# Inflows of a selective scan on GpSimd: two tiles of channels in one instruction

## The reference

```python
delta = jax.nn.softplus(jnp.einsum('blr,dr->bld', dt_r, dt_proj_w) + dt_proj_bias)
A = -jnp.exp(A_log)
def step(h, inp):
    delta_t, B_t, C_t, x_t = inp
    dA = jnp.exp(delta_t[..., None] * A)
    h = h * dA + (delta_t * x_t)[..., None] * B_t[:, None, :]
    y_t = jnp.einsum('bdn,bn->bd', h, C_t)
    return (h, y_t)
```

## Time and profile before

| | us |
|---|---|
| median of 3 runs | 2214.0 |
| lowest and highest run | 2208.6, 2216.2 |
| span of the profiled execution | 2212.1 |
| scan stage in it (`mamba`) | about 60 to 1310 |
| VectorE busy in the span | 1611.7 |
| TensorE busy in the span | 1779.5 |
| GpSimd busy in the span | 1009.2 |
| ScalarE busy in the span | 793.1 |

### The profile page before, as it was taken

How to read it: one execution, slowest core, us unless ns; L and a number is a source line. 1 busy time by engine, 2 the same in 40 slices (tenths; PEclk the granted TensorE clock), 3 DMA queues, 4 the chain that set the end, 5 groups by cost and what they waited for, 6 DMA issues and landing times. The chain is left out here.

```text
span 2212.1 us, 31372 instructions
## 1 busy us (share of the span) xinstructions
PE 1779.5 (80%) x8084; PEld 1285.4 (58%) x8084; DVE 1611.7 (73%) x2184; ACT 793.1 (36%) x1172; POOL 1009.2 (46%) x777
## 2 busy tenths in 40 slices
PE   3778767687676876768866668979997999999998
PEld 3345544454434554445543435657786999999997
DVE  0369999999989999899998834335763566655664
ACT  0444555445464553645545401211001233332332
POOL 1057547676576764767756532000001444433443
PEclk9989879798897997879978888999998999999999
DMA  5111101111101120011201042221121656666564
GB/s 135 69 29 64 53 25 35 39 58 56 29 30 40 54 64 24 30 40 49 69 25 30 24 162 85 95 106 57 58 79 44 163 124 165 162 146 164 143 161 82
DMA packets 81603, 169.61 MB, mean 77 GB/s; under 512 B 22459, under 2 KB 27467, under 8 KB 77979
## 3 DMA queue, kind: packets, MB, share of 16 engines
q1 hardware_dynamic: 57360, 116.06, 15.6%
q0 software_dynamic: 17856, 44.85, 10.4%
q10 hardware_dynamic: 6187, 6.37, 1.1%
HBM read 261.62 MB, written 39.24 MB: 136 GB/s over the span
## 5 line engine op out<-in xcount | busy, mean ns | idle before, releaser
L789 POOL TENSOR_TENSOR dbx<-u,b_all 128x512 f32<-128x512 f32 x512 | 642.2, 1278 | 350.5 <-DVE h L687 345.2
L687 DVE TENSOR_TENSOR_SCAN h<-da,dbx 128x512 f32<-128x512 f32 x512 | 596.2, 1203 | 40.2 <-ACT da L587 40.2
L587 ACT ACTIVATE da<-delta,a_neg 128x504 f32<-128x504 f32 x512 | 347.9, 684 | 474.1 <-DVE h L687 469.2
L427 PE MATMUL hT<-ident,h 128*128 128x128 f32 x2048 | 313.5, 313 | 229.6 <-DVE h L687 229.0
L427 PEld LDWEIGHTS hT<-ident,h 128*128 128x128 f32 x2048 | 274.8, 163 | 342.9 <-issue 337.6
L700 DVE SCALAR_TENSOR_TENSOR yacc<-hT,c_now,yacc 128x512 f32<-128x512 f32 x480 | 331.4, 732 | 4.3 <-PE hT L427 4.2
L334 PE MATMUL bank<-hid,w_in 128*128 128x512 f32 x608 | 291.4, 627 | 7.6 <-ACT hid L467 7.6
L1921 POOL DMA_INDIRECT out<-y,slots_kept x76 | 135.6, 1784 | 226.4 <-issue 158.1
L334 PEld LDWEIGHTS bank<-hid,w_in 128*128 128x128 f32 x608 | 120.4, 207 | 137.0 <-issue 128.1
L1554 POOL DMA_DIRECT2D slots_kept<-lists_kept x1 | 0.6, 577 | 331.2 <-DVE lists_kept L1508 331.2
L394 PE MATMUL bank<-w_out,skip 128*128 128x512 f32 x320 | 147.7, 609 | 2.5 <-DVE skip L659 2.5
(11 more groups left out here) (234 smaller groups left out, 3312.7 us busy)
## 6 DMA issues: line engine op xcount, KB each, us to landing
w_up_kept<-in_up_T SPq DMA_DIRECT2D x76, 1408.0 KB, 6.1
w_dn_kept<-in_dn_T SPq DMA_DIRECT2D x76, 768.0 KB, 7.4
b_all<-bt_scratch SPq DMA_DIRECT2D x128, 256.0 KB, 3.2
x_in<-in_x_pad ACTq DMA_DIRECT2D x21, 256.0 KB
res<-in_x_pad SPq DMA_DIRECT2D x20, 256.0 KB, 3.7
x_scratch<-res SPq DMA_DIRECT2D x20, 256.0 KB, 3.4
w_in<-in_in_T SPq DMA_DIRECT2D x8, 512.0 KB, 4.7
x_in<-x_scratch SPq DMA_DIRECT2D x4, 1024.0 KB, 5.3
```

Source lines behind the costliest of these rows:

```text
L427: mm = nc.tensor.transpose(hT[t][:, d * P:(d + 1) * P], h[:, m % RING, d, t * P:(t + 1) * P], ident[:])
L587: nc.scalar.activation(out[:, :, 1:], rows[:, :, 1:], ACT.Exp, scale=a_neg[:, d, n:n + 1]) \
L687: nc.vector.tensor_tensor_scan(h[:, n % RING, i, :], da[i % RING][:], dbx[:, i, :], 0.0, ALU.mult, ALU.add).then_inc(scan_done, 1)
L789: nc.gpsimd.tensor_tensor(dbx[:, i, :], u[:, d, :], b_all[:, m % RING, :], ALU.mult) \
```

## The change

One GpSimd instruction now makes the inflows of two neighbouring tiles of channels, 128x1024 columns: u of two tiles, times b_all repeated over both (`broadcast_to`, no copy is made). Per step two such instructions take the place of four. Each waits until the scans of the step before are done for both of its tiles, and at n = 0 until u of both is there. It adds 2 to dbx_made when it is done, so the semaphore's values mean what they meant, and no other engine's code changes.

```diff
+PAIR = 2
@@ inflow
                 if n == 0:
-                    pool.wait_ge(u_ready, j * DT + d + 1)
+                    pool.wait_ge(u_ready, j * DT + d + PAIR)
                 if i == 0:
                     pool.wait_ge(b_full[m % RING], j * (16 * STEPS // RING) + 16 * (m // RING + 1))
-                pool.wait_ge(scan_done, j * SCANS + HT * m + i + 1)
-                nc.gpsimd.tensor_tensor(dbx[:, i, :], u[:, d, :], b_all[:, m % RING, :], ALU.mult) \
-                    .then_inc(dbx_made, 1)
+                pool.wait_ge(scan_done, j * SCANS + HT * m + i + PAIR)
+                both = b_all[:, m % RING, :].unsqueeze(1).broadcast_to([P, PAIR, BLK])
+                nc.gpsimd.tensor_tensor(dbx[:, i:i + PAIR, :], u[:, d:d + PAIR, :], both, ALU.mult) \
+                    .then_inc(dbx_made, PAIR)
@@ the loop
                 for m in range(STEPS):
-                    for i in range(HT):
+                    for i in range(0, HT, PAIR):
                         inflow(j, *divmod(m, NST), i)
```

## The result

| | us |
|---|---|
| changed kernel, median of 4 runs | 2295.8 (2291.5 to 2300.3) |
| kernel before, beside it, median of 4 runs | 2214.3 (2208.6 to 2216.2) |
| ratio | 1.038 (95% interval 1.035 to 1.040) |
| spans of the profiled executions | 2298.0, before 2212.1 |

The change costs 82 us; 72 were forecast (2286 against 2296). Between the first and the last scan of the block loop the two traces differ by 83 of the 86 us of their spans, so the loss lies in the scan stage.

A forecast was written before the change was run, and what follows sets the result against it. VectorE was taken as the bound in the scan stage. Stalls of 19.4 us per block less 1.4 absorbed by waits gave 18.0, over four blocks 72 us, hence 2286 us, range 2253 to 2318.

The forecast's parts named there:

- What bounds: Scan stage: VectorE sets the pace, GpSimd's inflows lie beside its work, and VectorE never waits for dbx.
- The lock: A VectorE instruction with two SBUF inputs meeting a GpSimd TENSOR_TENSOR stands until its end, then needs 0.55 us.
- three-operand instructions: Rival: L625 and L633 share with GpSimd and don't stand; 5.4 us per block, 2236 us; chance 8%.
- a lock that falls between the tiles: Rival: GpSimd gives way in the middle of the pair, so stalls shrink; 2198 us; chance 6%.
- The price of the pair: One 128x1024 inflow on GpSimd takes 2.37 us, where two of today's take 2.51 us.
- the first three lines of the table: Stalls behind the last additions: 0.99 us in each of 11 steps, 0.63 in four, 0.52 in two.
- m = 31: Last step of a block: GpSimd itself waits for the next block's u, so nothing changes; 0 us.
- m = 0: Block's first scans, with L659 meeting the pairs and c_now's copy ending 0.1 us earlier: +1.4 us.
- What falls into waits: Stalls absorbed by waits VectorE has anyway, at m = 7 and m = 17: 1.4 us per block.
- m = 16 and 17: The 1.18 us wait at m = 17 takes 0.9 of m = 16's stall; 1.1 us left for both.
- m = 6 and 7: The 0.5 us stall at m = 6 falls into m = 7's wait for da; 1.0 us for both.
- m = 25: A step of the block loop where no loss was forecast: 0 us.

The follow-up runs named there:

- the kernel with each piece placed: The change, with VectorE's convolutions between scan 2 and scan 3 (but m = 16), L633 and make_u right behind scan 3, and m = 0 reordered: 2198.8 us, ratio 0.992.
- single inflows, pieces placed: The kernel before, its single inflows kept, with VectorE's two-SBUF pieces and m = 0 in the fastest kernel's order: 2231.1 us, ratio 1.007.
- the pair's waits and single instructions: The change's waits for both scans of a pair, but two 128x512 inflow instructions behind them instead of one of 128x1024: 2240.0 us, ratio 1.011.

## Why the prediction was right, point by point

**What bounds.** Right. VectorE's order set the pace. In the changed kernel its waits in the block loop are these, in the columns of the earlier trace rows:

```profile
DVE h L687 <- ACT da L587: 32.0, 6, 8.9
DVE yacc L700 <- PE hT L427: 7.4, 8, 1.2
DVE h L687 <- POOL dbx L790: 3.0, 2, 1.5
DVE c_now L718 <- issue: 0.8, 3, 0.3
```

The 3.0 us for dbx are two waits at m = 7 where da was late just as long (da done at 502.66, dbx at 502.74 in the second block); I had said there would be none.

**The lock.** Right, for three-operand instructions too, which closes that rival: L633 1.84 us, the first L625 1.84 at most steps. The rival of a lock that falls between the tiles would have shown 0.7 us. The Trainium skill, "SBUF — State Buffer", section "Who interferes with whom", calls the ports that the two engines share an exclusive lock: whoever issues first gets them for its whole instruction. The lengths agree (VectorE ends 0.55 to 0.56 us after GpSimd instructions of 1.27, 2.36 and 4.53 us), and so does the order: in the kernel with each piece placed, a lone L633 that began right behind scan 3, 0.23 to 0.27 us ahead of the pair, took 667 to 707 ns, and the pair took 2.66 us instead of 2.36.

**The price of the pair.** 2.37 us forecast, 2.36 measured. The piece ended 0.05 us later than forecast in each step: GpSimd followed scan 3 by 0.14 us, not 0.09, and L633 ended 0.56 us after the pair, not 0.55. In the first three lines of the table this is 0.65 us per block.

**m = 31, forecast "nothing changes".** Wrong, by 1.25 us per block. I had read the earlier trace rows as GpSimd waiting for u. But u of tiles 0 and 1 is long there; the first pair of the next block starts at once behind L764, and only the second waits for the u of tile 3, which comes just ahead of c_now's copy. The copy (L718) and the make_u ahead of it (L647) in the kernel before, and then the same place in the changed kernel:

```profile
692.84 0.68 DVE L647 TENSOR_TENSOR u<-delta,xc 128x512 f32<-128x512 f32 x1
695.85 1.18 DVE L718 COPY c_now<-c_next 128x64 f32<-128x64 f32 x1 [2.34 <-issue]
```

```profile
735.34 2.34 POOL L790 TENSOR_TENSOR dbx<-u,b_all 128x1024 f32<-128x1024 f32 x1
738.45 2.34 POOL L790 TENSOR_TENSOR dbx<-u,b_all 128x1024 f32<-128x1024 f32 x1 [0.77 <-DVE u L647]
...
735.47 2.77 DVE L647 TENSOR_TENSOR u<-delta,xc 128x512 f32<-128x512 f32 x1
738.49 2.36 DVE L718 COPY c_now<-c_next 128x64 f32<-128x64 f32 x1 [0.25 <-issue]
```

L647 stands 2.1 us longer, but that is hidden: in the kernel before VectorE sat idle 2.34 us behind it, on the way back to the top of the loop (the "issue" of the earlier trace rows), and now only 0.25. The copy behind it, of 64 columns, takes 2.36 us where it took 1.18: the forecast, under m = 0, had it end 0.1 us earlier. With only tiles 2 and 3 paired the step lost 1.0 us, with only tiles 0 and 1 nothing: it is the second pair.

**What falls into waits.** m = 16 and 17 came out at 0.9 for 1.1: the wait for da at m = 17 (1.3 us on average) was used up, but for 0.2 us in one block. At m = 6 and 7 nothing was absorbed in two of four blocks, and at m = 25 the additions waited 0.7 to 1.2 us for hT in all four blocks, where before only one had such a wait (0.5 us). I had taken TensorE's pace as given. Granted clock, third last column, from 130 to 1250 us, before and changed:

```profile
130.00:1250.00 1120.00, 821.96 (x3409) 507.22 (x3408) 1071.00 (x1242) 562.77 (x844) 733.67 (x586) 0.86 0.14 43
```

```profile
130.00:1250.00 1120.00, 793.72 (x3184) 496.27 (x3183) 1086.78 (x1160) 515.68 (x778) 642.41 (x304) 0.82 0.13 40
```

and the seven microseconds of m = 25 in the second block, before and changed:

```profile
633.00:640.00 7.00, 7.00 (x24) 2.64 (x23) 7.00 (x9) 4.35 (x8) 6.10 (x6) 0.76 0.11 37
```

```profile
670.00:677.00 7.00, 6.70 (x16) 2.62 (x16) 7.00 (x9) 4.44 (x7) 5.91 (x3) 0.63 0.11 39
```

The transposes (L427) with which TensorE resumed at m = 25, before and changed:

```profile
632.82 1.32 PE L427 MATMUL hT<-ident,h 128*128 128x128 f32 x8 [4.27 <-DVE h L687]
```

```profile
670.30 1.97 PE L427 MATMUL hT<-ident,h 128*128 128x128 f32 x8 [4.27 <-DVE h L687]
```

In those 7 us TensorE had 0.63 instead of 0.76 of its 2.4 GHz, after the same 4.27 us without work. The eight transposes took 0.65 us more, the next eight began 6.92 us after them instead of 6.21, and the additions then waited 0.66 us for hT. The same shows at m = 6 of this block, where the wait for da at m = 7 was not shortened: the eight transposes ahead of L325 took 1.97 us at a granted clock of 0.50, before 1.28 us at 0.78, and ScalarE's copy of hid, which stands ahead of da, waits for L325. With a slower VectorE, TensorE has less to do per us, and it spent more time at its lower level of 1.2 GHz. That this makes up the 0.8 us at m = 25 and the 0.4 at m = 7 is what the rows suggest; no run held the clock fixed. In the kernel with only tiles 2 and 3 paired, whose mean clock was 0.82 too, m = 25 lost 0.2 us, so the moment at which the clock dips counts, not the mean alone.

The sum, 18.0 forecast and 21.1 measured per block: +1.25 at m = 31, +0.8 at m = 25, +0.4 at m = 7, +0.25 at m = 0, +0.65 by the size of the stalls, -0.2 at m = 17.

## What to carry to other kernels

When an elementwise job is put on GpSimd beside a VectorE that is the bound, ask of each GpSimd instruction what VectorE runs during it. Here every VectorE instruction with both inputs in SBUF that started inside a GpSimd TENSOR_TENSOR waited for its end, so a merged instruction that saves 0.15 us of an idle engine cost 1.0 us per meeting. Give VectorE's work with an input in PSUM the time of the long instruction, and its two-SBUF work the hole behind it; and before a piece is moved, look at which other engine used the pause that it made.

## What the runs showed of the hardware

- A GpSimd TENSOR_TENSOR took 1.27 us for 512 columns, and 2.36 and 4.53 us for 1024 and 2048 with one input repeated over the tiles. Two TENSOR_TENSORs saved 0.15 us by being one.
- A VectorE copy of 128x64 from SBUF to SBUF (L718) is held up like the instructions with two SBUF inputs: 2.36 us beside a pair, 0.18 us alone in the first block of the changed kernel. A VectorE copy or TENSOR_SCALAR with its input in PSUM is not (L641 0.21 us, L697 0.73 us, both beside an inflow).
- GpSimd is held up in turn: where a VectorE instruction with two SBUF inputs had begun 0.15 to 0.35 us before it, most inflows took 1.69 to 1.73 us instead of 1.27 (single inflows, pieces placed), and a pair 2.66 instead of 2.36.
- The way back to the top of the loop, GpSimd: its first inflow of a block began 1.74 us after the work ahead of it, and at once (735.34, no idle time shown) in the changed kernel. It does not go by the number of inflows: the kernel with the pair's waits and single instructions has as many as the kernel before, and began at once too. What these two share is a shorter program with fewer waits (1409 entries of GpSimd in the trace, waits counted, before 1673). The two kernels that reorder VectorE's pieces and keep all 1673 have the gap, 1.5 to 1.8 us. The Trainium skill, "Runtime: NRT & Kernel Launch", section "Instruction fetch mechanics", says that a taken branch to code outside a window of two pages of instructions must fetch it first. A loop that has come to fit into that window would explain it; no run here shows the fetch itself.
- The way back, VectorE: in all kernels with its old order the copy L718 began 3.0 to 3.3 us after the start of the last L647, whether that one took 0.68 or 2.77 us, so a stall there is hidden. In the fastest kernel it was 2.1 us, with as many instructions; the runs don't say why. Its idle time, 7.3 us over three blocks in the kernel before, is 1.9 there, in part because its last L647 took 1.48 us instead of 0.68.
